# Preln attention and quantised feed-forward on one core: group 0's sums, the reciprocals and the products with them on GpSimd, and the first head outputs loaded in four pieces

## The chip, the cores and the metric

One core of a Trainium2 chip. The metric is the device time of the kernel in microseconds (us), the median of several executions. The core has TensorE (PE in the profile), VectorE (DVE), ScalarE (ACT), GpSimd (POOL), SyncE (SP), which issues all the DMAs here, and 16 DMA engines.

## The reference, cut to what matters

```python
x = residual                               # (2, 2048, 256)
xn = layernorm(x)
q, k, v = (einsum('bse,neh->bsnh', xn, W) + b for each of three W, b)      # 16 heads of 64
scores = where(q_idx < k_idx, 1e-10, q . k / 8)     # masked places count, with 1e-10
probs = softmax(scores)
x = x + einsum('bqnh,nhe->bqe', probs @ v, W_output) + Bias_output
h = layernorm(x)                           # then three blocks:
y = gelu(layernorm(qlora_linear(h))); h = qlora_linear(y) + h
out = x + h
```

A masked score is not minus infinity but 1e-10. So the denominator and the numerator have a masked part each: the number of keys after a query, and the sum of their values, times the weight of a masked place.

## The kernel before

Three stages follow one another, each a block of its own with its own semaphores: layernorm and weights, attention, feed-forward.

**Attention** works on N = 16 pairs of heads (2 batches of 8 pairs). A pair has 4 groups of 512 queries, in the order 3, 2, 1, 0, and each group its tiles of two blocks of 128 keys (`TILES`): 8, 6, 4 and 2, together NT = 20 (tiles 0 to 7, 8 to 13, 14 to 17, 18 and 19). The last two tiles of a group lie on the diagonal and are narrower (512 and 384 columns, then 256 and 128; for group 3 they stand at tiles 2 and 3). For a tile and each of the two heads, TensorE makes scores (lines 822 to 827), ScalarE takes the exponential into `probs` (line 961; three buffers, so tile t + 3 needs tile t's back), TensorE multiplies with the values into `ps_o` (line 843), and GpSimd adds the probs up over the keys in `acc` (lines 724 and 731). A tile's scores are issued one tile ahead of its product.

The order on each engine is written out by hand. A pair has 120 slots, 6 to a tile, and TensorE fits the next pair's work between its matmuls by slot (`between`): projections (`PROJ_SLOT`), score maxima (`MAX_AT`) and the list `FIN`: transposed values ("vt"), transposed maxima ("mt"), and "den", the sum of `acc` over the partitions by a matmul with ones (line 793). These share three banks of PSUM, `ps_bg`. For group 0 no engine adds up first: at slot 120 `denominators` sums the probs of both tiles directly with ones (line 799). GpSimd's loop ends with the last tile of group 1. In the last pair VectorE does the additions (`add_last`).

From the sums to the output, for each group: ScalarE copies the sums to `den_rows` (926); SP fetches them into the square form `den_sq` of 32 x 32 (`take_den`, 555); VectorE adds the masked part and takes the reciprocal (`invert`, 1043 and 1047) at `INVERT_SLOT`; SP writes it out (`put_inverse`, 561) and spreads it over the partitions (`spread_inverse`, 570); VectorE multiplies the numerator with it (`normalise`, 1055) at `NORMAL_SLOT`; SP stores (`store_heads`, 576). `take_numerator` (1035) frees `ps_o`; `num` has two buffers. GpSimd also makes the masked numerator (`masked_part`, 703) and denominator (694). SP's order is one fixed list.

**Feed-forward** works on 8 chunks of 512 rows, two at a time. SP loads the output weights `wo` (1 MB), then chunk 0's head outputs (`o_in`, 2 MB) and residual, chunk 1's, and 28 small loads of weights and biases. `heads_out(0)` and `heads_out(1)` (line 1304, 64 matmul instructions each) come first; GpSimd adds the output bias to the residual (`add_bias`) once all the small loads are there.

## Time and profile before

| what | us |
|---|---|
| median of 3 runs | 2429.66 (2426.53 to 2451.3) |
| profiled execution, its own time | 2423.18 |
| its span, first to last instruction | 2421.4 |
| TensorE busy | 2247.3 |
| VectorE / ScalarE / GpSimd busy | 1421.2 / 813.6 / 1240.8 |

The attention stage lies between 106 us (first projections) and 2045 us, the feed-forward from 2051 us to the end. Busy time of TensorE is the union of its matmuls, which overlap; its idle time before an instruction is put down to what released it.

### The profile page before, as it was taken

What the parts mean: (1) busy time and instruction counts of PE and PEld (TensorE: products, weight loads), DVE (VectorE), ACT (ScalarE), POOL (GpSimd) and SP (SyncE); (2) the same over time, 40 slices, a digit from 0 to 9 for tenths busy, and PEclk for the clock granted to TensorE, in tenths of its full rate; (3) what the DMA queues carried; (4) which work ended last, traced back from release to release, by engine and by line L of the source; (5) the groups of instructions that cost most, each with busy time, mean ns of one, the idle gap of its engine ahead of it and who ended that gap; (6) DMA issues with size and microseconds to landing.
All of it is one profiled execution on the core that took longest, in us unless ns stands there. A gap on an engine that the chain in (4) does not pass through costs nothing. (4 is left out here: it accounts for less than half of the span.)

```text
span 2421.4 us, 30652 instructions
## 1 busy us (share of the span) xinstructions
PE 2247.3 (93%) x10080; PEld 1149.0 (47%) x10080; DVE 1421.2 (59%) x3782; ACT 813.6 (34%) x1166; POOL 1240.8 (51%) x1139
## 2 busy tenths in 40 slices
PE   4389999999999999999999999999999995899987
PEld 3224444444444444444444444444444442767764
DVE  3585665656665656565656565656565763265664
ACT  1113434343434343434334344434343442011111
POOL 0106666667676757575757584858584810111110
PEclk8569999999999999999999999999999998899998
DMA  4564363635354445545453536353535332521100
GB/s 122 160 157 108 83 159 80 156 95 140 102 134 111 125 122 147 130 110 134 101 140 95 151 90 152 95 147 99 147 95 141 88 93 73 193 87 61 61 18 18
DMA packets 205356, 273.61 MB, mean 113 GB/s; under 512 B 69201, under 2 KB 86801, under 8 KB 205201
## 3 DMA queue, kind: packets, MB, share of 16 engines
q1 hardware_dynamic: 205200, 271.67, 42.8%
q8 instruction: 82, 1.34, 0.2%
q14 instruction: 74, 0.60, 0.1%
HBM read 176.69 MB, written 94.63 MB: 112 GB/s over the span
## 5 line engine op out<-in xcount | busy, mean ns | idle before, releaser
L731 POOL TENSOR_TENSOR acc<-acc,probs 128x512 f32<-128x512 f32 (+1 forms) x900 | 980.7, 1125 | 377.6 <-ACT probs L961 377.6
L961 ACT ACTIVATE probs<-ps_s 128x1024 f32<-128x1024 f32 (+2 forms) x640 | 549.4, 897 | 332.5 <-PE ps_s L824 157.2
L1011 DVE TENSOR_REDUCE partial<-ps_bg 128x1 f32<-128x512 f32 x768 | 490.3, 684 | 202.8 <-PE ps_bg L766 202.4
L822 PE MATMUL ps_s<-qq,kk 128*128 128x512 f32 (+3 forms) x1280 | 573.2, 448 | 18.8 <-ACT probs L961 18.8
L843 PE MATMUL ps_o<-probs,v 128*64 128x512 f32 (+3 forms) x2560 | 537.8, 541 | 0.0
L824 PE MATMUL ps_s<-qm,kl 128*128 128x512 f32 (+3 forms) x1280 | 467.1, 365 | 0.0
L757 PE MATMUL ps_bg<-xs,w_in 128*128 128x512 f32 x768 | 364.5, 599 | 20.8 <-DMA xs<-xn_turned 18.9
L822 PEld LDWEIGHTS ps_s<-qq,kk 128*128 128x128 f32 x1280 | 243.5, 190 | 202.4 <-issue 154.3
L766 PE MATMUL ps_bg<-k_bf,q_bf 64*128 64x512 bf16 (+3 forms) x1280 | 274.5, 364 | 20.2 <-DVE split L988 10.4
L1008 DVE CUSTOM_DVE_ANT_0 junk<-ps_bg,mask_q 128x512 bf16<-128x512 f32 (+3 forms) x512 | 230.7, 485 | 104.7 <-issue 103.5
L843 PEld LDWEIGHTS ps_o<-probs,v 128*64 128x64 f32 x2560 | 155.3, 136 | 229.9 <-issue 206.0
L824 PEld LDWEIGHTS ps_s<-qm,kl 128*128 128x128 f32 x1280 | 242.5, 189 | 38.8 <-issue 21.5
L766 PEld LDWEIGHTS ps_bg<-k_bf,q_bf 64*128 64x128 bf16 x1280 | 73.6, 93 | 355.0 <-issue 295.1
L910 ACT ACTIVATE split<-ps_bg,bias 128x512 fp32r<-128x512 f32 x128 | 88.0, 688 | 440.8 <-PE ps_bg L757 440.6
L724 POOL TENSOR_TENSOR acc<-probs 128x512 f32<-128x512 f32 x90 | 113.3, 1280 | 237.5 <-ACT probs L961 237.5
L988 DVE SCALAR_TENSOR_TENSOR split<-ps_bg,bias,split 128x512 fp32r<-128x512 f32 x128 | 94.6, 739 | 202.0 <-ACT split L910 201.3
L757 PEld LDWEIGHTS ps_bg<-xs,w_in 128*128 128x128 f32 x768 | 141.6, 191 | 131.0 <-issue 117.5
L1271 POOL TENSOR_TENSOR c_rstd<-c_var,c_minus_half 128x4 f32<-128x4 f32 x32 | 35.2, 1101 | 269.5 <-DVE c_var L1435 269.5
L1304 PE MATMUL c_ps<-c_wo,c_o_in 128*128 128x256 f32 x512 | 114.9, 384 | 28.5 <-DMA c_o_in<-heads_turned 28.5
L703 POOL TENSOR_TENSOR masked_num<-v_from,e 128x512 f32<-128x512 f32 x64 | 76.9, 1201 | 112.5 <-DVE num L1035 110.9
L1304 PEld LDWEIGHTS c_ps<-c_wo,c_o_in 128*128 128x128 f32 x512 | 98.7, 194 | 42.4 <-issue 28.7
L827 PE MATMUL ps_s<-never_above,ident_bf 128*128 128x128 bf16 x512 | 118.0, 230 | 0.0
(102 smaller groups left out, 1659.0 us busy)
## 6 DMA issues: line engine op xcount, KB each, us to landing
high_and_low<-split SPq DMA_DIRECT2D x128, 512.0 KB, 5.8
qq<-high_and_low SPq DMA_DIRECT2D x64, 512.0 KB, 4.7
kk<-high_and_low SPq DMA_DIRECT2D x128, 256.0 KB, 5.5
qm<-high_and_low SPq DMA_DIRECT2D x64, 256.0 KB, 6.4
kl<-high_and_low SPq DMA_DIRECT2D x64, 256.0 KB, 6.8
e<-masked_weights SPq DMA_DIRECT2D x128, 128.0 KB, 3.0
scale<-inverse_sums SPq DMA_DIRECT2D x128, 128.0 KB, 2.9
heads_turned<-o_out SPq DMA_DIRECT2D x64, 256.0 KB, 3.1
```

The source lines that it names most:

```text
L724: g.tensor_tensor(acc[h][:, group % 2, :], pr[:, 0:CH], pr[:, CH:2 * CH], ALU.add).then_inc(added, 1)
L731: g.tensor_tensor(acc[h][:, group % 2, q0:q0 + w], acc[h][:, group % 2, q0:q0 + w], probs[h][:, probs_slot(i, t), at:at + w], ALU.add).the ...
L757: mm = pe.matmul(bank("proj", j, u), w_in[:, s, m, :], xs[:, c, s, :], start=(s == 0), stop=(s == halves - 1))
L766: pe.matmul(bank("max", j, n, h)[:, 0:w], q_bf[HEAD[h], qb * P:(qb + 1) * P], k_bf[HEAD[h], CH * u:CH * u + w], start=True, stop=True).the ...
L822: pe.matmul(out, kk[:, h, kb * P:(kb + 1) * P], qq[:, h, q], start=True, stop=False, skip_group_check=True)
L824: mm = pe.matmul(out, kl[:, h, kb * P:(kb + 1) * P], qm[:, h, q], start=False, stop=not diagonal, skip_group_check=True)
L827: mm = pe.matmul(ps_s[:, h, at:at + P], ident_bf[:, :], never_above[:, :], start=False, stop=True, skip_group_check=True)
L843: mm = pe.matmul(ps_o[64 * h:64 * h + 64, q0:q0 + w], v[:, kb, 64 * h:64 * h + 64], probs[h][:, probs_slot(i, t), at:at + w], start=first, ...
L961: nc.scalar.activation(probs[h][:, probs_slot(i, t), 0:width], ps_s[:, h, 0:width], ACT.Exp, scale=SCORE_SCALE).then_inc(p_ready, 1)
L1008: e.tensor_tensor_reduce(junk[:, k, 0:w], of, mask_q[:, CH - w:CH], 1.0, 3 * NEVER, ALU.add, ALU.max, to).then_inc(max_read, 1)
L1011: e.reduce_max(to, of, AX.X).then_inc(max_read, 1)
L1304: mm = pe.matmul(ps_y[L][:, t, :], o_in[b][:, a, t * P:(t + 1) * P], wo[:, a, :], start=(a == 0 and t % 2 == 0), stop=(a == n_pairs - 1), ...
```

## The change

- Group 0's probs are added up by GpSimd like those of the others, in `acc[h][:, 0]`: a copy of the first 128 columns, an addition of 384, then the second tile's 256 and 128. The two matmuls with ones for it move from slot 120 to slot 14 of the next pair. Line 799 goes. In the last pair VectorE does these additions.
- `invert` and `normalise` move from VectorE to GpSimd, between its tiles (`INVERT_TILE`, `NORMAL_TILE`; from 20 on they mean tiles of the next pair). The reciprocal becomes a power of -1.
- `num` has a third buffer.
- SP's list is put in another order around them; `fin_before` gives way to a table `number` of the same counts.
- In the feed-forward, `wo` and the first two chunks' head outputs are loaded in `PIECES` = 4 pieces of two head pairs with a semaphore each, and TensorE multiplies piece by piece. The output bias has its own semaphore, for which alone `add_bias` waits. TensorE waits for the small loads only ahead of the first linear layer.

```diff
-    for k in range(min(t, LAST_TILE[1] + 1)):
-        n += 2 if k == FIRST_TILE[TILES[k][0]] else 4
+    for k in range(t):
+        n += 2 if TILES[k][0] and k == FIRST_TILE[TILES[k][0]] else 4
...
-FIN = [("vt", 0, 3), ("vt", 3, 50), ("den", 3, 60), ("mt", 3, 72), ("vt", 2, 86), ("mt", 2, 96), ("den", 2, 98),
-       ("den", 1, 110), ("vt", 1, 113), ("mt", 1, 114), ("mt", 0, 119), ("den", 0, SLOTS)]
-NFIN = len(FIN)
...
-INVERT_SLOT = {3: 68, 2: 106, 1: 118, 0: SLOTS + 8}
-NORMAL_SLOT = {3: 77, 2: 115, 1: SLOTS + 7, 0: SLOTS + 17}
+INVERT_TILE = {3: 11, 2: 17, 1: NT, 0: NT + 4}
+NORMAL_TILE = {3: 13, 2: NT, 1: NT + 2, 0: NT + 6}
...
                     if i:
+                        install_chunk(i, 0)
+                        put_inverse(i - 1, 1)
                         spread_inverse(i - 1, 1)
-                        install_chunk(i, 0)
-                        take_den(i - 1, 0)
+                        store_heads(i - 1, 2)
                         install_max(i, 0)
-                        store_heads(i - 1, 1)
                     if more:
                         keep_split(i + 1, 3)
-                    if i:
-                        put_inverse(i - 1, 0)
                     load_masked(i)
                     spread_masked(i, 3)
                     if i:
+                        store_heads(i - 1, 1)
+                    if more:
+                        keep_split(i + 1, 2)
+                    if i:
+                        take_den(i - 1, 0)
+                    spread_masked(i, 2)
+                    if more:
+                        keep_split(i + 1, 1)
+                    if i:
+                        put_inverse(i - 1, 0)
                         spread_inverse(i - 1, 0)
                     if more:
-                        keep_split(i + 1, 2)
-                    spread_masked(i, 2)
+                        keep_split(i + 1, 0)
                     if i:
                         store_heads(i - 1, 0)
-                    if more:
-                        keep_split(i + 1, 1)
-                        keep_split(i + 1, 0)
...
-                    store_heads(i, 2)
...
-                    put_inverse(i, 1)
...
+                put_inverse(N - 1, 1)
                 spread_inverse(N - 1, 1)
+                store_heads(N - 1, 2)
                 take_den(N - 1, 0)
-                store_heads(N - 1, 1)
                 put_inverse(N - 1, 0)
                 spread_inverse(N - 1, 0)
...
+                def invert(i, group):
+                    n = nth(i, group)
+                    pool.wait_ge(den_sq_in, START + 32 * (n + 1))
+                    pool.wait_ge(masked_den_ready, START + i + 1)
+                    pool.wait_ge(inverse_ready, START + n)
+                    g.tensor_tensor(total[:, :, :], den_sq[:, :, :], masked_den[:, i % 2, group], ALU.add
+                                    ).then_inc(total_ready, 1)
+                    pool.wait_ge(consts, START + 1)
+                    pool.wait_ge(total_ready, START + n + 1)
+                    pool.wait_ge(inverse_kept, START + 16 * n)
+                    g.tensor_tensor(inverse[:, :, :], total[:, :, :], minus_one[:, :, :], ALU.pow).then_inc(inverse_ready, 1)
+                def normalise(i, group):
+                    n = nth(i, group)
+                    pool.wait_ge(scale_in[group % 2], START + 32 * (2 * i + (3 - group) // 2 + 1))
+                    pool.wait_ge(num_ready, START + n + 1)
+                    pool.wait_ge(o_stored[group % 2], START + 16 * (2 * i + (3 - group) // 2))
+                    g.tensor_tensor(o_out[:, group % 2, :], num[:, n % 3, :], scale[:, group % 2, :], ALU.mult
+                                    ).then_inc(o_ready, 1)
+                def between_tiles(i, t):
+                    for c in (2, 1, 0):
+                        if i and t == INVERT_TILE[c] - NT:
+                            invert(i - 1, c)
+                        if i and t == NORMAL_TILE[c] - NT:
+                            normalise(i - 1, c)
+                    for c in (3, 2):
+                        if t == INVERT_TILE[c]:
+                            invert(i, c)
+                    if t == NORMAL_TILE[3]:
+                        normalise(i, 3)
...
                 for i in range(N - 1):
                     n = 0
-                    for t in range(LAST_TILE[1] + 1):
+                    for t in range(NT):
                         group, tile = TILES[t]
...
-                            if t == MASKED_TILE[c]:
...
+                        between_tiles(i, t)
...
+                        if t == FIRST_TILE[group] and (i or group < 2):
+                            pool.wait_ge(fin_written, START + number["den", i if group < 2 else i - 1, (group + 2) % 4])
+                        if t == FIRST_TILE[0]:
+                            for h in range(2):
+                                pr = probs[h][:, probs_slot(i, t)]
+                                g.tensor_copy(acc[h][:, 0, 0:P], pr[:, 0:P]).then_inc(added, 1)
+                                g.tensor_tensor(acc[h][:, 0, P:CH], pr[:, P:CH], pr[:, CH:2 * CH - P], ALU.add
+                                                ).then_inc(added, 1)
+                            n += 4
+                            continue
...
-                masked_denominators(N - 1)
-                for c in GROUPS:
-                    masked_part(N - 1, c)
+                for t in range(NT):
+                    if t == MASKED_DEN_TILE:
+                        masked_denominators(N - 1)
+                    between_tiles(N - 1, t)
+                for t in range(NT, NT + 7):
+                    between_tiles(N, t - NT)
...
-                    if group:
-                        if i < N - 1:
-                            pe.wait_ge(added, START + POOL_OPS * i + pool_ops_before(LAST_TILE[group] + 1))
-                        else:
-                            pe.wait_ge(added_last, START + pool_ops_before(LAST_TILE[group] + 1))
-                        for h in range(2):
-                            mm = pe.matmul(to[64 * h:64 * h + 64, :], ones64[:, :], acc[h][:, group % 2, :],
-                                           start=True, stop=True, skip_group_check=True)
+                    if i < N - 1:
+                        pe.wait_ge(added, START + POOL_OPS * i + pool_ops_before(LAST_TILE[group] + 1))
                     else:
-                        for t in range(FIRST_TILE[0], NT):
-                            for kb, q0, w, at in TILES[t][1]:
-                                for h in range(2):
-                                    mm = pe.matmul(to[64 * h:64 * h + 64, q0:q0 + w], ones64[:, :],
-                                                   probs[h][:, probs_slot(i, t), at:at + w],
-                                                   start=(kb == 0), stop=(kb == 3), skip_group_check=True)
+                        pe.wait_ge(added_last, START + pool_ops_before(LAST_TILE[group] + 1))
+                    for h in range(2):
+                        mm = pe.matmul(to[64 * h:64 * h + 64, :], ones64[:, :], acc[h][:, group % 2, :],
+                                       start=True, stop=True, skip_group_check=True)
...
-                    between(i, SLOTS)
+                denominators(N - 1, 0)
...
                                         act.wait_ge(added_last, START + pool_ops_before(user % NT + 1))
-                                    if user % NT >= FIRST_TILE[0]:
-                                        act.wait_ge(fin_written, START + fin_before(i, 0))
...
                                                  scale=SCORE_SCALE).then_inc(p_ready, 1)
-                        if i and t == 0:
...
                     dve.wait_ge(p_ready, START + 2 * NT * (N - 1) + 2 * t + 2)
                     if t == FIRST_TILE[group]:
-                        if group == 1:
-                            dve.wait_ge(fin_written, START + fin_before(N - 1, fin_index("den", 3)) + 1)
-                        else:
-                            dve.wait_ge(fin_written, START + fin_before(N - 1, 0))
+                        dve.wait_ge(fin_written, START + number["den", N - 1 if group < 2 else N - 2, (group + 2) % 4])
+                    if t == FIRST_TILE[0]:
+                        for h in range(2):
+                            pr = probs[h][:, probs_slot(N - 1, t)]
+                            e.tensor_copy(acc[h][:, 0, 0:P], pr[:, 0:P]).then_inc(added_last, 1)
+                            e.tensor_tensor(acc[h][:, 0, P:CH], pr[:, P:CH], pr[:, CH:2 * CH - P], ALU.add
...
+                def load_piece(g, p):
+                    of = pairs_of(p)
+                    if g == 0:
+                        sp.dma_start(wo[:, of, :], w_out.rearrange("(a p) d -> p a d", p=P)[:, of]
+                                     ).then_inc(piece_loaded[g][p], 16)
+                    sp.dma_start(o_in[g][:, of, :], ot.rearrange("b a c p t -> b c p a t")[g // 4, 3 - g % 4][:, of]
+                                 ).then_inc(piece_loaded[g][p], 16)
...
+                for g in range(2):
+                    for p in range(PIECES):
+                        load_piece(g, p)
+                    if g == 0:
+                        sp.dma_start(b_out_row[:, :], b_out.rearrange("(o d) -> o d", o=1).to_broadcast([P, D])
+                                     ).then_inc(b_out_loaded, 16)
+                    sp.dma_start(x_in[g][:, :, :], x[g]).then_inc(x_loaded[g], 16)
                 for dst, src in loads:
                     sp.dma_start(dst, src).then_inc(w_loaded, 16)
...
+                def heads_out_by_piece(g):
+                    for p in range(PIECES):
+                        pe.wait_ge(piece_loaded[g][p], START + (32 if g == 0 else 16))
+                        for a in range(n_pairs)[pairs_of(p)]:
+                            for t in range(4):
+                                mm = pe.matmul(ps_y[g][:, t, :], o_in[g][:, a, t * P:(t + 1) * P], wo[:, a, :],
+                                               start=(a == 0 and t % 2 == 0), stop=(a == n_pairs - 1),
+                                               skip_group_check=True)
+                    mm.then_inc(y_summed[g], 1)
...
                         heads_out(c, (0, 1))
+                    if i == 0:
```

## Rows read from the trace of the kernel before

**Rows 1.** The page, part 1: busy us, share of the span, instructions of each engine
```profile
PE 2247.3 (93%) x10080; PEld 1149.0 (47%) x10080; DVE 1421.2 (59%) x3782; ACT 813.6 (34%) x1166; POOL 1240.8 (51%) x1139
```
**Rows 2.** Waits: TensorE's from 178 to 2050 us; VectorE's for DMA, whole trace
```profile
PE ps_s L822 <- ACT probs L961: 18.8, 17, 1.2
PE ps_bg L766 <- DVE split L988: 10.4, 15, 0.7
...
DVE total L1043 <- DMA den_sq<-den_rows: 140.6, 31, 6.8
```
**Rows 3.** Busy us by stretch (PE, PEld, DVE, ACT, POOL), granted clock, DMA share, GB/s
```profile
875.00:991.00 116.00, 113.97 (x524) 53.62 (x522) 70.06 (x189) 46.24 (x66) 75.69 (x69) 1.00 0.55 141
```
**Rows 4.** Line 799's instructions; timeline of TensorE at two groups of sums (start, us)
```profile
L799 PE MATMUL ps_bg<-probs,ones x256: 272/432/644, 295.9 to 2033.2; 128*64 128x512 f32 x32, 128*64 128x384 f32 x32, 128*64 128x256 f32 x32, 128*64 128x128 f32 x32
...
989.50 1.08 PE L793 MATMUL ps_bg<-acc,ones 128*64 128x512 f32 x4
990.51 0.33 PE L822 MATMUL ps_s<-qq,kk 128*128 128x128 f32 x1
...
1007.10 2.37 PE L799 MATMUL ps_bg<-probs,ones 128*64 128x512 f32 x16
1009.40 0.50 PE L822 MATMUL ps_s<-qq,kk 128*128 128x512 f32 x1
```
**Rows 5.** Groups of instructions by form: busy us, mean ns of one, idle before
```profile
L731 POOL TENSOR_TENSOR acc<-acc,probs 128x512 f32<-128x512 f32 x630 | 792.2, 1289 | 377.6 <-ACT probs L961 377.6
L731 POOL TENSOR_TENSOR acc<-acc,probs 128x384 f32<-128x384 f32 x90 | 88.5, 1006 | 0.0
L703 POOL TENSOR_TENSOR masked_num<-v_from,e 128x512 f32<-128x512 f32 x64 | 76.9, 1201 | 112.5 <-DVE num L1035 110.9 <-DMA e<-masked_weights 1.6
L996 DVE CAST k_bf<-split 128x512 bf16<-128x512 f32 x64 | 47.0, 734 | 0.0
L731 POOL TENSOR_TENSOR acc<-acc,probs 128x128 f32<-128x128 f32 x90 | 39.9, 465 | 0.0
L994 DVE CAST q_bf<-split 128x512 bf16<-128x512 f32 x64 | 31.6, 494 | 0.0
L134 POOL TENSOR_TENSOR a_rstd<-a_var_eps,a_minus_half 128x4 f32<-128x4 f32 x8 | 8.1, 1011 | 72.1 <-DVE a_var_eps L159 72.1
```
**Rows 6.** Timeline of GpSimd from group 1's first tile (idle time before in brackets)
```profile
977.23 2.53 POOL L724 TENSOR_TENSOR acc<-probs 128x512 f32<-128x512 f32 x2 [1.53 <-ACT probs L961]
982.61 4.98 POOL L731 TENSOR_TENSOR acc<-acc,probs 128x512 f32<-128x512 f32 x4 [2.86 <-ACT probs L961]
...
988.60 6.61 POOL L731 TENSOR_TENSOR acc<-acc,probs 128x512 f32<-128x512 f32 x8
```
**Rows 7.** Timeline and landing of den_sq, 990 to 996 us; group 1's sums on TensorE
```profile
991.24 1.21 SPq L555 DMA_DIRECT2D den_sq<-den_rows  x2
...
DMA to landing us min/median/max: 1.7/1.7/1.7
...
998.15 1.08 PE L793 MATMUL ps_bg<-acc,ones 128*64 128x512 f32 x4
```
**Rows 8.** Timeline at the end of attention
```profile
2031.17 2.32 PE L799 MATMUL ps_bg<-probs,ones 128*64 128x512 f32 x16
...
2034.44 1.13 SPq L570 DMA_DIRECT2D scale<-inverse_sums  x2
...
2037.87 0.69 DVE L1055 TENSOR_TENSOR o_out<-num,scale 128x512 f32<-128x512 f32 x1 [4.69 <-DMA scale<-inverse_sums]
...
2045.01 0.34 SPq L576 DMA_DIRECT2D heads_turned<-o_out  x1
```
**Rows 9.** Timeline at the start of the feed-forward
```profile
2051.08 0.41 SPq L1235 DMA_DIRECT2D c_wo<-in_L_attn_W_output  x1
...
2062.01 29.36 PE L1304 MATMUL c_ps<-c_wo,c_o_in 128*128 128x256 f32 x128 [28.52 <-DMA c_o_in<-heads_turned]
...
2096.14 1.94 PE L1316 MATMUL c_ps<-c_ident,c_z 128*128 128x128 f32 x8 [4.77 <-DVE c_z L1444]
```

More of the change, by code:

```diff
@@ L326, in background @@
             order += [(kind, pair_of(i, kind, c), c) for kind, c, at in FIN
-                      if at == n and pair_of(i, kind, c) < n_pairs_in_all]
-    first, users, counts = {}, [], {"proj": 0, "max": 0, "fin": 0}
+                      if at == n and 0 <= pair_of(i, kind, c) < n_pairs_in_all]
+    order.append(("den", n_pairs_in_all - 1, 0))
+    first, users, number, counts = {}, [], {}, {"proj": 0, "max": 0, "fin": 0}
     for use in order:
@@ L334, in background @@
             users.append((kind, counts[kind]))
-    return first, users
+        number[use] = counts[kind]
+    return first, users, number
 FIN_FIRST = [("mt", 3), ("mt", 2), ("mt", 1), ("mt", 0), ("vt", 3), ("vt", 2), ("vt", 1)]
-NFIRST = len(FIN_FIRST)
 def attention(nc, xnt, w_qkv, b_qkv, parts, max_kept, kept, inverses, ot):
@@ L941, in _ @@
                 act.wait_ge(consts, START + 1)
[L942 to L943 removed]
+                for kind, c in FIN_FIRST:
+                    evacuate(0, kind, c)
                 for i in range(N):
```

130 lines of the change are left out of this document (48 added, 82 removed).

## The prediction, made before the changed kernel had run

> **What bounds the kernel now.** I read the page first: PE is busy for 93% of the span, POOL for 51% [rows 1]. Busy is not proof of a bound, so next the waits of PE over the attention stage, from 178 to 2050 us: of those 1870 us PE waits about 19 for ScalarE, once in a pair, and 10 for VectorE [rows 2]. Nobody keeps PE waiting; it is the list of its matmuls that takes the time. The table by stretches shows the same for 116 us in the middle of the stage: PE 113.97 us busy at full granted clock (1.00, 2.4 GHz), VectorE 70, GpSimd 75.7 [rows 3]. A pair lasts (1007.1 - 295.9) / 6 = 118.5 us, from the first start of the matmuls that add up group 0 to those of pair 6 [rows 4]. So in attention a microsecond taken off PE is a microsecond off the time, 15 times over (the last pair has no next pair to prepare and ends in a tail of its own), and a microsecond that PE must wait is one lost. In the feed-forward the start counts: PE stands still for 28.5 us, until 2062.0, for the first head outputs [rows 9].
>
> **Part 1, group 0's sums leave PE.** Before, line 799 makes them with 16 matmul instructions a pair; these begin at 1007.10 and the next scores at 1009.40, 2.30 us. The other groups' sums (line 793, 4 instructions) begin at 989.50 and the next scores at 990.51, 1.01 us [rows 4]. The new group 0 is of that second kind. PE gains 1.29 us a pair, 15 x 1.29 = **-19.4 us**. They also move from the end of the pair to slot 14 of the next, where they wait for GpSimd's last addition of group 0: by my reckoning below it is done within some 6 us of the pair's end, and PE comes there about 20 us after it. This wait costs nothing. ScalarE's copy of the sums moves along.
>
> **Part 2, what GpSimd gets.** By the rows of one form [rows 5] an addition takes 1289 ns at 512 columns and 465 at 128: 2.15 ns a column and 0.19 us for the rest. In each pair are new: two copies of 128 columns (no row has one; between 0.19, the fixed part, and 0.465, an addition; 0.4 taken), two additions each of 384, 256 and 128 columns (1.01, by the line 0.74, and 0.47): 5.2 us. Four products like line 703's, 4 x 1.20 = 4.8. Four additions of 32 columns at 0.19 + 32 x 0.00215 = 0.26: 1.0. And four reciprocals as a power of -1 over 32 columns. Together 11.0 us + 4 P, with P the time of one power.
>
> **P is the open term.** The only power in the trace has 4 columns and takes 1.01 us (line 134) [rows 5], of which an ordinary instruction would need 0.20; 0.81 us is the power's own. If all of it is a fixed cost, P is 1.0 us; if it goes with the columns, 0.20 us each, P is 0.19 + 32 x 0.205 = 6.7 us. These are the ends. I take **P = 2 us**, near the lower: 0.8 us spent on 4 columns is more easily a start-up and a few steps in flight than 32 times a lone step, but no row has a second width, and this is the weakest point of the sum. At 2 us GpSimd's load is 77 + 19 = 96 of 117 us, and it fits on average. What counts is where it queues.
>
> **Part 3, the place where a late GpSimd meets PE.** PE adds up group 1 (line 793 again) at slot 110, 998.15 in pair 6 [rows 7], and now waits there for an engine with more to do. The new step ahead of it is the reciprocal of group 2, set before tile 17's additions. Its input: SP issues the two copies of the sums at 991.24, the second about 0.6 later, and they land after 1.7 us [rows 7], at 993.5. GpSimd's run of 8 additions from 988.60 takes 6.61 us [rows 6]; its first four, tile 16's, cost two of 512 and two of 384 columns, 4.4 us back to back, and end at 993.0. Then 0.26 + P, then tile 17's four, 2.2 us: done at 993.5 + 0.26 + P + 2.2 = 996.0 + P. Against 998.15 this leaves **2.1 us for P**, with a tenth lost to each of the two hand-overs some 2.0. At P = 2 the wait is just covered; every microsecond beyond is lost 15 times. Further up, at tile 11, stands group 3's reciprocal and at tile 13 a product: 1.5 us + P more before GpSimd's two idle stretches of 1.53 and 2.86 us [rows 6], 4.39 in all. So for P up to 2.9 it has caught up before tile 16; beyond that this excess is added to the other.
>
> The remaining ones lie at tiles 20 to 26, that is 0 to 6 of the next pair. ScalarE needs tile t's probs free at tile t + 3, three tiles or some 17 us later; GpSimd may be blocked there for the landing of group 1's sums (VectorE now waits up to 6.8 us for such landings [rows 2]) and still meet that. The new waits on the queues: behind GpSimd's wait for a landing stand its own additions only; SP's wait for the reciprocal now comes after the installation of chunk 0, so that is issued sooner, and what stands behind it (the next split chunk, needed at tile 3, 20 us on) has room. store_heads and the third numerator buffer take a wait for the product off VectorE; it was none that PE saw, so nothing is gained. VectorE loses its 4 x 0.7 us of products and its waits for landings: nothing either, it is not the bound.
>
> **Part 4, the tail.** Before: PE's last sums begin at 2031.17 and the last store is issued at 2045.01; one spread-out of the inverse to the product takes 2037.87 - 2034.44 = 3.43 us [rows 8]. After, PE finishes 1.3 us sooner, but in SP's queue the fetch of group 0's sums stands behind group 1's reciprocal, its spread-out and a store, and reciprocals and products are slower. Followed with 1.4 us for addition and reciprocal: group 1's put at 2035.0, spread at 2036.8, group 0's sums fetched at 2038.3, in at 2040.9, inverted at 2042.8, spread at 2044.6, in at 2048.1, product 1.2: last store at 2049.3, +4.3 us. With P = 2 each of the two reciprocals adds 1: **+6.3 us**.
>
> **Part 5, the heads in pieces.** Before, one load of 1 MB and one of 2 MB, the first issued at 2051.08, have to be in before PE starts at 2062.01 [rows 9]: 3 MB in 10.9 us, of which some 8 are transfer (0.39 MB a us) and some 3 latency. A quarter is 2 us of transfer: PE can start at about 2056, 6 us sooner. It needs some 3.5 us for a piece at full clock and twice that at the half clock at which it comes out of the idle stretch; pieces land every 2 us, so it never waits again. Its 128 instructions, 29.4 us, are the same [rows 9], and everything behind (PE's first transpositions at 2096) moves with them: **-6 us**, between -2 (if the later load of chunk 2, issued behind more small loads, becomes late) and -7. The bias's own load and the later wait for the weights are needed so that VectorE can follow; they cost nothing, as VectorE starts on chunk 0 only when PE is done with it.
>
> **The sum.** -19.4 + 0 + 6.3 - 6.0 = **-19.1 us** against the profiled execution, whose own time is 2423.2 (span 2421.4). The median of the runs shown is 2429.7, 6.5 more; taken off that: **2410 us**, -0.8%. Changes within 1% (24 us) are about what a measurement of this kernel can't tell from none, and this forecast lies just inside.
>
> **A rule against the change.** Line 703's product takes GpSimd 1.20 us [rows 5], VectorE's takes 0.69 [rows 8]. The Trainium skill, "GPSIMD Engine Reference", section "Engine selection", says that two-input elementwise work belongs on VectorE, GpSimd being about twice as slow: the rows agree, at 1.7. By that rule the four products would cost a pair 2 us more; by the waits only the tail's last one is on the path.
>
> **Rivals.**
> *The power goes with its columns*, P = 6.7. For it: 4 x 0.2 explains the one row fully. Against: nothing but my guess of a start-up. Then PE waits at slot 110 of each pair 4.7 + 3.8 = 8.5 us; it decides from P = 3 on, where the wait (1.1) eats the 1.3 gained. Time: -19.4 + 15 x 8.5 + 4.3 + 2 x 5.7 - 6 = +118: 2548 us, slower.
> *The power lies between*, P from 2.3 to 3.5: waits of 0.3 to 2.1 us a pair, +5 to +32, tail +1 to +3 more: 2416 to 2445, no difference.
> *VectorE gets slower.* Its casts of the same size take 494 and 734 ns on average [rows 5], and the slower one stands where PE waits 0.7 us a pair for VectorE's split. The Trainium skill, "GPSIMD Engine Reference", section "Specifications", says the two engines share their SBUF interfaces, with contention when VectorE has two SBUF inputs; the rows of casts fit a contention but don't show it. With GpSimd busy for a quarter more of the time, this 0.24 us could strike at two or three more places where PE is close behind: +1 to +1.5 us a pair, +15 to +22. 2425 to 2432, no difference.
>
> **Chances.** Forecast 0.62, own range 2400 to 2422; power between 0.15; power by columns (P above 3.5) 0.15; slow VectorE 0.08. The range that leaves out 2 in 10 takes the forecast's, both no-difference rivals and omits the power by columns: 2398 to 2445. Faster by over 1% (under 2405.4): the forecast with the copies and waits at their lower ends, and the median's 6 us above the profiled execution gone, 0.30. Slower by over 1%: the power by columns and the upper end of "between" with a slow VectorE, 0.19. Within: 0.51.
>
> **What would show it.** Line 799 gone, the interval between the sums of one group in neighbouring pairs down from 118.5 to 117.2; the power's row, which decides: under 2 us and PE's waits stay near 2 us a pair; above, a new row PE ps_bg <- POOL acc at line 793, as many microseconds as P exceeds 2. The last store of attention 20 us (before: 13.8) after the start of PE's last sums. First head matmul 5 us after SP's first load instead of 11. The prediction is wrong if the power is long, if tile 16's additions end late, or if VectorE's split makes PE wait more than 1 us a pair.

## The result, and the profile after

The changed kernel takes **2612.9 us** (median of 4 runs, 2593.8 to 2637.0) against 2432.7 of the kernel before in the same series: ratio 1.070, 95% interval 1.059 to 1.081. 2410 was forecast, in a range of 2398 to 2445: wrong in sign and size. One of the four runs, the 2637.0, was in a slower state; the ratio leaves it out and compares 2602.4, the median of the other three. The profiled execution has 2602.4 us, a span of 2600.6 and a mean granted clock of 0.937 (before: 2421.4 and 0.968).

The page, part 1, of the changed kernel, beside [rows 1]:

```profile
PE 2276.7 (88%) x9888; PEld 1150.9 (44%) x9888; DVE 1374.1 (53%) x3599; ACT 814.8 (31%) x1166; POOL 1753.3 (67%) x1451
```

TensorE has 192 instructions fewer and yet 29 us more busy time: its instructions took longer, so the clock fell. GpSimd has 512 us more. Its groups by form (busy us, mean ns of one, idle time before) show what was added:

```profile
L716 POOL TENSOR_TENSOR inverse<-total,minus_one 32x32 f32<-32x32 f32 x64 | 347.5, 5430 | 8.5
L724 POOL TENSOR_TENSOR o_out<-num,scale 128x512 f32<-128x512 f32 x64 | 84.2, 1316 | 28.9 <-DMA scale<-inverse_sums 28.9
...
L757 POOL TENSOR_TENSOR acc<-probs 128x384 f32<-128x384 f32 x30 | 29.6, 986 | 0.0
L711 POOL TENSOR_TENSOR total<-den_sq,masked_den 32x32 f32<-32x32 f32 x64 | 16.1, 251 | 87.2 <-DMA den_sq<-den_rows 87.2
L756 POOL COPY acc<-probs 128x128 f32<-128x128 f32 x30 | 8.4, 280 | 0.0
```

The first row is P: **5.43 us**, not 2. Product, copy and small addition are within 0.12 us of what was estimated. TensorE's waits, beside [rows 2] (in total, times, longest):

```profile
PE ps_bg L833 <- POOL acc L771: 93.4, 15, 6.6
PE ps_s L855 <- ACT probs L993: 50.7, 33, 2.2
...
PE ps_bg L808 <- DVE partial L1038: 17.1, 20, 9.5
```

Three rows, three losses. The first is the one the prediction named as its test: TensorE at the sums' line waits for GpSimd. The second was 18.8 us, 17 times, before; a second wait per pair has come. The third has one wait of 9.5 us in it. The timeline of GpSimd and of TensorE where the first one falls (start, us; idle time before in brackets):

```profile
1184.11 4.43 POOL L771 TENSOR_TENSOR acc<-acc,probs 128x512 f32<-128x512 f32 x4
1188.50 0.24 POOL L711 TENSOR_TENSOR total<-den_sq,masked_den 32x32 f32<-32x32 f32 x1
1188.87 5.43 POOL L716 TENSOR_TENSOR inverse<-total,minus_one 32x32 f32<-32x32 f32 x1
1194.28 2.21 POOL L771 TENSOR_TENSOR acc<-acc,probs 128x256 f32<-128x256 f32 x4
```
```profile
1196.64 1.97 PE L833 MATMUL ps_bg<-acc,ones 128*64 128x512 f32 x4 [6.58 <-POOL acc L771]
1204.93 0.47 PE L855 MATMUL ps_s<-qq,kk 128*128 128x512 f32 x1 [1.16 <-ACT probs L993]
...
1210.81 0.50 PE L855 MATMUL ps_s<-qq,kk 128*128 128x512 f32 x1 [2.17 <-ACT probs L993]
```

In order: tile 16's additions, group 2's sum and power, tile 17's additions, and then at once group 1's sums on TensorE. That is the order of Part 3. The sums take 1.97 us where they took 1.08. The table by stretches tells why (TensorE's busy time, granted clock, DMA share, GB/s):

```profile
1187.00:1190.00 3.00, 3.00 (x24) 1.00 0.00 0
1190.00:1193.00 3.00, 0.06 (x1) 1.00 0.00 0
1193.00:1196.60 3.60, 0.00 (x0) 0.50 0.01 1
1196.60:1203.00 6.40, 6.36 (x19) 0.50 0.83 223
1203.00:1209.00 6.00, 4.49 (x26) 0.98 0.36 71
```

Some 3 us into the wait the granted clock has gone from 1.00 to 0.50 (2.4 to 1.2 GHz), and it stays there for 6.4 us of work after it: 3.2 us lost behind a wait of 6.6. This is one of the dearer pairs. Behind the 15 waits for GpSimd the work at half clock lost 1.8 to 3.4 us each, 2.6 on average. The shorter wait of 2.17 us at the turn of the pair was followed by half clock in 6 of 15 pairs, 1.7 us lost each time, 0.7 a pair on average.

A **period**, from group 1's sums to those of the next pair, is 118.2 to 118.9 us before and 127.9 to 130.7 after, with one of 139.0. For a typical pair: 6.4 (wait) + 2.6 + 0.7 (clock, in the two places) + 0.9 (the new wait at the turn of the pair, less the matmuls saved; first experiment) = 10.6, and 118.5 + 10.6 = 129.1. Over the whole: the last sums start 170.0 us later (2201.21 for 2031.17), from there to the feed-forward's first load it takes 34.6 us for 19.9 (+14.7), and from that load to the end of the span 364.9 for 370.3 (-5.4). 170.0 + 14.7 - 5.4 = 179.3; the two spans differ by 179.2.

### The profile page after: what moved, and what is told of

Read it like the earlier page. It is cut to its first block and busy times, and to the rows that moved or that the text cites. A ratio compares the mean times of both kernels' runs of the same rounds, so it can differ in the third digit from the quotient of the medians.

```text
span 2600.6 us, 30428 instructions
## 1 busy us (share of the span) xinstructions
PE 2276.7 (88%) x9888; PEld 1150.9 (44%) x9888; DVE 1374.1 (53%) x3599; ACT 814.8 (31%) x1166; POOL 1753.3 (67%) x1451
## 5 line engine op out<-in xcount | busy, mean ns | idle before, releaser
L771 POOL TENSOR_TENSOR acc<-acc,probs 128x512 f32<-128x512 f32 x960 | 1016.9, 1089 | 238.3 <-ACT probs L993 238.2
L855 PE MATMUL ps_s<-qq,kk 128*128 128x512 f32 (+3 forms) x1280 | 581.1, 454 | 50.7 <-ACT probs L993 50.7
L876 PE MATMUL ps_o<-probs,v 128*64 128x512 f32 (+3 forms) x2560 | 554.0, 555 | 0.0
L857 PE MATMUL ps_s<-qm,kl 128*128 128x512 f32 (+3 forms) x1280 | 472.4, 369 | 0.0
L799 PE MATMUL ps_bg<-xs,w_in 128*128 128x512 f32 x768 | 369.7, 607 | 19.1 <-DMA xs<-xn_turned 19.1
L716 POOL TENSOR_TENSOR inverse<-total,minus_one 32x32 f32<-32x32 f32 x64 | 347.5, 5430 | 8.5
L799 PEld LDWEIGHTS ps_bg<-xs,w_in 128*128 128x128 f32 x768 | 142.7, 192 | 129.1 <-issue 118.8
L833 PE MATMUL ps_bg<-acc,ones 128*64 128x512 f32 x256 | 82.5, 726 | 94.6 <-POOL acc L771 93.4
L960 ACT COPY den_rows<-ps_bg 128x512 f32<-128x512 f32 x64 | 37.5, 587 | 235.0 <-PE ps_bg L833 229.6
```

What stands on the lines that cost most here:

```text
L716: g.tensor_tensor(inverse[:, :, :], total[:, :, :], minus_one[:, :, :], ALU.pow).then_inc(inverse_ready, 1)
L771: g.tensor_tensor(acc[h][:, group % 2, q0:q0 + w], acc[h][:, group % 2, q0:q0 + w], probs[h][:, probs_slot(i, t), at:at + w], ALU.add).the ...
L799: mm = pe.matmul(bank("proj", j, u), w_in[:, s, m, :], xs[:, c, s, :], start=(s == 0), stop=(s == halves - 1))
L855: pe.matmul(out, kk[:, h, kb * P:(kb + 1) * P], qq[:, h, q], start=True, stop=False, skip_group_check=True)
L857: mm = pe.matmul(out, kl[:, h, kb * P:(kb + 1) * P], qm[:, h, q], start=False, stop=not diagonal, skip_group_check=True)
L876: mm = pe.matmul(ps_o[64 * h:64 * h + 64, q0:q0 + w], v[:, kb, 64 * h:64 * h + 64], probs[h][:, probs_slot(i, t), at:at + w], start=first, ...
```

## The experiments

Twelve kernels besides the changed one, in three series with the kernel before running beside each (its medians there: 2443.7, 2437.6 and 2435.1). "Power" says what takes the reciprocal. "Period" is the usual one, in us. Three kernels leave something out: multiply_for_power takes no reciprocal at all, power_16_columns and power_16_scan_first only that of one head in two.

| run | power | time, us | ratio to before (95%) | period |
|---|---|---|---|---|
| changed kernel | GpSimd, 32 columns | 2612.9 | 1.070 (1.059 to 1.081) | 129 |
| recip_on_vector | VectorE's reciprocal | 2441.3 | 0.998 (0.996 to 1.001) | 119.3 |
| all_on_vector | VectorE's reciprocal | 2453.8 | 1.005 (1.003 to 1.008) | 120.2 or 121.9 |
| pieces_only | VectorE's reciprocal | 2437.7 | 0.998 (0.996 to 1.001) | 118.2 to 122.1 |
| power_later | GpSimd, 32 columns | 2643.8 | 1.081 (1.076 to 1.086) | 131 to 137 |
| multiply_for_power | none | 2436.8 | 1.000 (0.998 to 1.002) | 119.3 |
| power_16_columns | GpSimd, 16 | 2620.4 | 1.073 (1.069 to 1.077) | 130 to 134 |
| power_on_128_lanes | GpSimd, 8 | 2480.2 | 1.016 (1.013 to 1.020) | 119.5 to 121 |
| mt0_moved | VectorE's reciprocal | 2425.4 | 0.995 (0.993 to 0.997) | 118.4 |
| power_16_scan_first | GpSimd, 16 | 2522.6 | 1.037 (1.033 to 1.041) | 124 to 126 |
| lanes_scan_first | GpSimd, 8 | 2475.6 | 1.016 (1.012 to 1.020) | 120.5 or 122.1 |
| mt0_slot8 | VectorE's reciprocal | **2406.1** | **0.989 (0.985 to 0.992)** | 117.2 |
| lanes_scan_mt8 | GpSimd, 8 | 2439.5 | 1.000 (0.998 to 1.003) | 118.4 to 120 |

### First series: which part costs it

**recip_on_vector**: only the reciprocals (addition and reciprocal) go back to VectorE. Three stand at their old slots; group 0's stands at slot 24 of the next pair instead of 8, because its sums now come at slot 14.

```diff
-INVERT_TILE = {3: 11, 2: 17, 1: NT, 0: NT + 4}        # GpSimd: power
+INVERT_SLOT = {3: 68, 2: 106, 1: 118, 0: SLOTS + 24}  # VectorE: e.reciprocal
```

> The changed kernel with the addition and the reciprocal of invert back on VectorE (its RECIPROCAL, at the old slots); the products stay on GpSimd. Theory 1, the long power: the power of 32 columns takes 5.4 us at GpSimd and makes PE wait 6.6 us a pair at group 1's sums, and the wait brings the half clock. Without it that row of waits is gone, the clock is 1.00 all through attention and the span falls by 160 us or more. Theory 2, the lost cover: taking line 799 away uncovers a wait of 2.2 us of PE for ScalarE at the pair's start, so of the 1.3 us that it was to bring nothing is left; then the span is 2421 + 15 x 0.9 - 5.5 (pieces) + 3 (tail) = 2432. If the cover was not lost: 2412. Theory 3, GpSimd has simply too much (its load and the shared use with VectorE): over 2460 even so.

2441.3 us: no row for GpSimd is left in TensorE's waits, and the loss is gone. The one row that stays is the second of the three:

```profile
PE ps_s L837 <- ACT probs L975: 50.1, 31, 2.2
```

Period 119.26, so 0.9 over before, where -1.3 was forecast. ScalarE's timeline at the turn of the pair, in this kernel:

```profile
1139.39 0.25 ACT L937 CAST rows<-ps_bg 8x128 fp32r<-8x128 f32 x1 [1.67 <-PE ps_bg L796]
1139.68 0.31 ACT L948 ACTIVATE rows<-rows 8x128 f32<-8x128 f32 x1
1140.02 0.40 ACT L951 ACTIVATE rows<-rows,masked_bias 8x128 f32<-8x128 f32 x1
1140.44 1.94 ACT L975 ACTIVATE probs<-ps_s 128x1024 f32<-128x1024 f32 x2
```

The row of maxima of group 0 ("mt" 0, slot 119) makes three small steps, 1.05 us, directly ahead of the exponentials that TensorE's next scores wait for. Before, TensorE was doing line 799's matmuls over just this time, 2.3 us at 1007.10 [rows 4].

**all_on_vector**: the products go back to VectorE too.

> As recip_on_vector, and the products back on VectorE as well: only group 0's sums stay on GpSimd, with the three buffers, SP's new order and the pieces. Theories 1 and 2: same as recip_on_vector within 3 us of span (2430), for the products were never what PE waited for. Theory 3: clearly faster than recip_on_vector, by 10 us or more.

A miss for all three theories: 1 and 2 had expected no difference, 3 a gain, and the kernel is 12 us slower than recip_on_vector. VectorE's product, two operands in SBUF, takes 1.08 us here (0.75 in the kernel before), and TensorE waits for maxima behind line 1009 for 9.5 us, 18 times (1.3 us, 4 times, in recip_on_vector). These 64 instructions, at these slots (group 1's and 0's are later than in the kernel before), are better off on GpSimd.

```profile
L1053 DVE TENSOR_TENSOR o_out<-num,scale 128x512 f32<-128x512 f32 x64 | 68.9, 1076 | 19.9 <-DMA scale<-inverse_sums 19.9
```

**pieces_only**: the kernel before with nothing but the new start of the feed-forward.

> The kernel before with the new feed-forward stage alone (output weights and head outputs of two chunks in four pieces). All theories: attention as before, span 2421.4 - 5.5 = 2416, PE's first head matmul 4.5 us after SP's first load (before: 10.9). If the pieces were part of the loss: above 2421.

First load to first matmul 5.0 us (before: 10.9), first load to the end 364.3 (370.3): -6.0. The forecast of Part 5 holds for this stage. In the medians it is -0.2%, within what can be told from none. The span expected, 2416, did not come: it is 2431.4, because the attention stage, which the edit does not touch, ended 15.5 us later than in the profile of the kernel before (periods of 118.2 to 122.1 for 118.2 to 118.9). The kernel before itself took 2433 to 2458 us in this series. So the span decides nothing here; the stretch of the feed-forward does.

**power_later**: the power of group 2 one tile later, behind tile 17's additions (`INVERT_TILE = {..., 2: 18, ...}`).

> The changed kernel with group 2's power one tile later, at tile 18 and so behind tile 17's additions, on which PE's sums of group 1 wait. Nothing else. Theory 1 (the place counts, not the load): PE's wait at group 1's sums falls from 6.6 to about 1 us a pair, the half-clock stretches go with it, span 2440 to 2470. Theory 3 (the load counts): GpSimd is as full as before, the wait only moves to ScalarE's probs, span above 2560.

A miss. The wait at the sums fell to 0.8 us at most, and these came for it:

```profile
PE ps_bg L808 <- DVE partial L1041: 62.9, 11, 10.8
PE ps_bg L808 <- DVE vt L1013: 49.4, 8, 8.8
```

TensorE waits for VectorE, and VectorE has no wait for GpSimd in this profile. It is VectorE's casts that are held up. Each takes 0.42 us as a rule; here 24 of them take 2.3 to 11.9, and all 128 together 242 us for 89 in the changed kernel. One of them, with GpSimd beside it and TensorE behind it:

```profile
1152.02 4.93 POOL L771 TENSOR_TENSOR acc<-acc,probs 128x512 f32<-128x512 f32 x4
1153.34 11.21 DVE L1024 CAST q_bf<-split 128x512 bf16<-128x512 f32 x1
1156.91 1.25 POOL L702 TENSOR_TENSOR masked_num<-v_from,e 128x512 f32<-128x512 f32 x1
1158.13 4.91 POOL L771 TENSOR_TENSOR acc<-acc,probs 128x512 f32<-128x512 f32 x4
1163.01 1.25 POOL L724 TENSOR_TENSOR o_out<-num,scale 128x512 f32<-128x512 f32 x1
```
```profile
1165.20 0.61 PE L808 MATMUL ps_bg<-k_bf,q_bf 64*128 64x512 bf16 x1 [10.78 <-DVE partial L1041]
```

The cast starts inside a run of GpSimd without a gap and ends at 1164.55, 0.3 us after the last of the rows shown; GpSimd's next and last instruction of the run, at 1164.22, has 32 partitions. The maxima stand behind it, and TensorE behind them. By these rows the new place of the power shifted GpSimd's runs onto the casts; no run with a gap at the casts was made to show it. When this run was planned, only the queue behind the old place had been looked at.

### Second series: is it the power's length?

**multiply_for_power**: `ALU.pow` becomes `ALU.mult` in the same place.

> The changed kernel with a multiplication by -1 in the place of the power in all four groups, at the same places of GpSimd's list; it leaves out the reciprocal, nothing else. The instruction should take 0.25 us, like the addition ahead of it, instead of 5.43. Theory 1 (the power's length alone makes TensorE wait at the sums of groups 2 and 1; the other 11 us of new GpSimd work fit): that wait falls from 6.6 us a pair to under 0.5, the half-clock stretches go with it, the pair's period falls from 129 to 119.3 us (118.4 of before plus the 0.9 us that TensorE now waits for ScalarE at the turn of the pair), and the time comes to 2435 to 2446, as in the run with the reciprocals on VectorE. Rival (GpSimd is overloaded whatever the power costs, or its hand-overs are what is late): a wait of 1 us or more a pair stays in the rows for GpSimd, and the time stays over 2455.

The reciprocal is left out; its place in the list stays. The instruction takes 0.253 us, the period is 119.27, and the time 2436.8 is within 5 us of recip_on_vector. GpSimd's other 11 us of new work a pair cost TensorE nothing. **The power's length is the loss**: by the two ratios, 1.070 and 1.000, some 170 us.

**power_16_columns**: the power over one head's 16 columns, a multiplication over the other's, whose reciprocal is left out.

> The changed kernel with the power over the first head's 16 columns only and a multiplication over the second head's 16: it leaves out the second head's reciprocal. If the power goes by its columns (1.01 us at 4, 5.43 at 32: 0.38 + 0.158 a column) the instruction takes 2.9 us, with the multiplication 3.2. GpSimd works without an idle stretch from group 3's reciprocal to group 2's in the changed kernel, so theory 1 (each microsecond of either power comes back at that wait until GpSimd has caught up) takes 2 x 2.2 off the 6.6 us wait: 2.1 us are left, too short for the clock to fall; period 121.5, time 2470 (2460 to 2480). Rival A (only group 2's own power counts, the other is caught up in idle time): 4.3 us stay, with the clock's loss a period of 125 and 2520 to 2550. Rival B (the power has a large fixed part or another law, so that 16 columns cost about as much as 32): the time stays over 2570.

The most instructive miss. The power takes 2.91 us and the wait at the sums is 31.7 / 15 = 2.1 us a pair, both as theory 1 had it, and still the kernel is as slow as with 32 columns. TensorE's first row of waits, and VectorE and GpSimd where its longest ones fall:

```profile
PE ps_bg L811 <- DVE partial L1041: 100.4, 28, 8.5
```
```profile
1197.97 0.85 POOL L774 TENSOR_TENSOR acc<-acc,probs 128x128 f32<-128x128 f32 x2
1198.41 9.86 DVE L1057 TENSOR_TENSOR_SCAN v_from<-ones_row,v_from,vt 128x512 f32<-128x512 bf16 x1
1198.79 2.48 POOL L767 TENSOR_TENSOR acc<-probs 128x512 f32<-128x512 f32 x2
1201.23 4.91 POOL L774 TENSOR_TENSOR acc<-acc,probs 128x512 f32<-128x512 f32 x4
1206.11 1.08 POOL L703 TENSOR_TENSOR masked_num<-v_from,e 128x512 f32<-128x512 f32 x1
```

VectorE's scan, 1.28 us in the kernel before (64 times, none over 1.29), takes **9.86**. It starts while GpSimd is busy and ends at 1208.27, 1.08 us after GpSimd's run ends at 1207.19. The maxima that TensorE needs stand behind it. 13 of the 15 scans at this slot are this long (9.03 to 10.34). In the changed kernel there is one, 11.32 us at 1430.89, again to 1.1 us after GpSimd's first idle moment: this is its pair of 139.0 us and its wait of 9.5. Yet there too all 15 start inside a run of GpSimd without a gap. Ten of them took 1.4 us and four 2.4 to 3.3, each let in between two of GpSimd's instructions, the second of which took 1.63 us for 0.72. So the run is needed for a long scan but doesn't bring one by itself. The shorter power shifted the run: in 10 of the 13 long cases the scan starts beside additions of 512 columns, in the changed kernel mostly beside those of 256. That this decides is not shown; the one long scan of the changed kernel starts like ten short ones.

Theory 1 also called a wait of 2.1 us "too short for the clock to fall". The waits of 2.17 us at the turn of the pair, followed by half clock in 6 of 15 pairs of the changed kernel, speak against that.

The Trainium skill, "SBUF — State Buffer", section "SBUF: two separate sides", says that the two engines share a pair of ports as an exclusive lock when VectorE has two SBUF inputs, held for a whole instruction. The trace agrees that the scan is held up, but not for one instruction: here it stood through seven more of them.

**power_on_128_lanes**: nothing left out, the denominators (total, inverse and the masked ones too) laid out as 128 partitions of 8 columns.

```diff
-        den_sq = sb("den_sq", [32, 2, 16])
+        den_sq = sb("den_sq", [P, 2, 4])
...
-den_rows[64 * h:64 * h + 1, :].rearrange("o (p e) -> o p e", e=16)
+den_rows[64 * h:64 * h + 1, :].rearrange("o (p e) -> o p e", e=4)
```

> The changed kernel with nothing left out, the denominators laid out as 128 partitions of 2 x 4 instead of 32 of 2 x 16, so that the power has 8 columns: 0.38 + 8 x 0.158 = 1.65 us instead of 5.43, if what counts is columns and not elements. Theory 1: GpSimd's wait at the sums is gone, the period falls to 119.3 and the time to 2435 to 2448. Rival (the power goes by elements, which are as many as before): 5.4 us and 2590 and more. Rival 2 (copies in 16-byte pieces land later): the power is short but GpSimd waits longer for the denominators and TensorE behind it 1 us or more a pair, 2455 to 2480.

```profile
L716 POOL TENSOR_TENSOR inverse<-total,minus_one 128x8 f32<-128x8 f32 x64 | 105.7, 1651 | 8.5
```

The same 1024 elements, 3.3 times faster: it goes by columns. But 2480, not 2448: three scans of about 9 us, twelve of 1.7 to 2.9, some with small waits behind, and a tail of 27.8 us where multiply_for_power has 19.5. Rival 2 has a point in the tail: SP's write of the inverse, in smaller pieces now, lands after 2.6 us (median; 1.4 in the changed kernel).

**mt0_moved**: recip_on_vector, with group 0's row of maxima turned at slot 4 of its own pair; SP's fetch of it moves along (not shown).

```diff
-       ("den", 1, 110), ("vt", 1, 113), ("mt", 1, 114), ("mt", 0, 119)]
+       ("den", 1, 110), ("vt", 1, 113), ("mt", 1, 114)]
-FIN = [("vt", 0, 3), ("den", 0, 14), ("vt", 3, 50), ("den", 3, 60), ("mt", 3, 72), ("vt", 2, 86), ("mt", 2, 96), ("den", 2, 98),
+FIN = [("vt", 0, 3), ("mt", 0, 4), ("den", 0, 14), ("vt", 3, 50), ("den", 3, 60), ("mt", 3, 72), ("vt", 2, 86), ("mt", 2, 96), ("den", 2, 98),
```

> On top of the run with the reciprocals on VectorE: the row of maxima of group 0 is turned at slot 4 of its own pair instead of slot 119 of the one before, so ScalarE no longer has its three small steps between the last exponentials of a pair and the first of the next. Theory (TensorE's new wait of 2.2 us a pair for probs at the turn is this chain, which the 2.3 us of group 0's sums used to cover): the wait at the turn is gone, the period falls from 119.3 to 117.2 us, and the time from 2441 to 2405 to 2412, the gain of 1.29 us a pair that was forecast for the sums plus what had been hidden behind them. Rival (the exponentials of the first tile are late for another reason, such as group 0's last scores or the conversion of V): the wait stays at 1 us or more and the time at 2425 to 2441.

Half: the wait went from 2.2 to 1.2 us, the period to 118.4. At slot 4 the three steps still stood directly ahead of the next exponentials, with a little more of TensorE's work beside them.

### Third series: the cures

**power_16_scan_first**: power_16_columns, and GpSimd waits at tile 14 until the scan is done.

```diff
+                        if t == FIRST_TILE[1]:
+                            pool.wait_ge(sums_ready, START + 4 * (i + 1) + 2)
```

> The run with the power over 16 columns (it leaves out the second head's reciprocal), and one wait more: before its first addition of group 1 (tile 14) GpSimd waits until VectorE's scan of V (128x512, set at slot 86) is done, which leaves a stretch without GpSimd work for the scan. In that run the scan took 9 to 10 us instead of 1.28 in 12 of 14 pairs, always while GpSimd went without an idle stretch from one instruction to the next, and ended about 1.1 us after GpSimd had stopped; TensorE then stood some 8 us for VectorE's maxima. Theory (VectorE's scan can't get through while GpSimd works without a break): the scan is back at 1.3 to 1.8 us, the waits for maxima fall from 100 to under 10 us, GpSimd reaches the sums about 1.3 us later than by the power alone, 3.4 us of wait a pair; period 122.7, time 2480 to 2510 instead of 2620. Rival (the long scan is a symptom, for example VectorE waits for something of TensorE's or ScalarE's, and GpSimd's load as such costs the time): scans stay long somewhere, or TensorE waits elsewhere, and the time stays over 2570.

```profile
L1059 DVE TENSOR_TENSOR_SCAN v_from<-ones_row,v_from,vt 128x512 f32<-128x512 bf16 x64 | 84.7, 1323 | 1.7
```
```profile
PE ps_bg L838 <- POOL acc L776: 44.1, 15, 3.6
...
PE ps_bg L813 <- DVE partial L1046: 1.0, 3, 0.3
```

GpSimd gets a wait more, and the kernel is some 90 us faster (ratio 1.037 for 1.073). The scans are at 1.3 us, the waits for maxima gone, 2.9 us a pair wait at the sums. A gap in GpSimd's run is enough to keep the scans short. The time is 13 us above the upper end expected, which had left out the clock: it took 30 us between 300 and 1900 us (table below).

**lanes_scan_first**: the same wait with the power on 128 x 8.

> The power on 128 partitions x 8 columns (1.65 us, nothing left out) and the same wait of GpSimd for the scan ahead of tile 14. Theory (the 40 us that this kernel still lost are three pairs with a scan of 9 us and small waits for maxima in the others): no scan over 1.8 us, all pairs at 119.3 to 120, 2437 to 2450, level with the run that multiplies. Rival (the scan's wait only moves the loss to the sums: GpSimd, held 1.3 us, comes late there): a wait for GpSimd of about 1 us a pair and 2455 to 2465.

The rival is right in kind: all scans at 1.28 us, 1.3 us a pair of wait at the sums instead. 2475.6 is no better than without. Periods are 120.5 or 122.1, and the 1.6 between them is a stretch of half clock at the turn of the pair, behind the wait of 2.17 us.

**mt0_slot8**: as mt0_moved, but slot 8, and SP fetches it behind the first split chunk.

> As the run with the row of maxima of group 0 turned in its own pair, but at slot 8 instead of slot 4, and its fetch by SP behind the first split chunk. At slot 4 ScalarE's three small steps still stood directly ahead of the exponentials that TensorE waits for (1.2 us a pair instead of 2.2). At slot 8 ScalarE has 5 us without work. Theory: this wait goes, only the 1.16 us stays that the kernel before has too; period 118.4 - 1.2 = 117.2, the forecast of the sums' own gain; 2405 to 2412. Rival (SP's queue, now held until slot 8, brings the split chunks and the masked weights late): the period stays at 118.4 or grows, with waits for DMA behind the split or at the masked denominators.

```profile
PE ps_s L840 <- ACT probs L978: 17.7, 16, 1.2
```

The second wait is gone, the period is 117.17, and **2406.1 us is 1.1% faster than before** (ratio 0.989, 0.985 to 0.992), the fastest kernel of this study, some 200 us ahead of the changed one. That Part 1's gain of 1.29 us a pair exists is shown; it needed the row of maxima out of the way.

**lanes_scan_mt8**: all on GpSimd as in the change, with the three cures.

> All on GpSimd as the change has it, with the three cures together: power on 128 x 8, GpSimd waiting for the scan ahead of tile 14, maxima of group 0 turned at slot 8 of their own pair. If the three losses are independent, the period is 117.2 to 117.8 and the time 2407 to 2420, faster than before by the forecast's amount. If GpSimd's load is itself a loss, it stays 1 us a pair or more behind the run with the reciprocals on VectorE.

2439.5, 33 us behind mt0_slot8: 1.3 us a pair at the sums (19.6, 15 times), some waits for maxima (5.8, 12 times), and a tail of 27.1 us for 20.2. In this kernel the reciprocals are better off on VectorE.

**What the clock takes.** For each kernel TensorE's windows of 1 us from 300 to 1900 us, added up: idle time, and half of the time that it was busy at half clock.

| kernel | TensorE idle, us | lost to half clock, us |
|---|---|---|
| before | 29 | 0 |
| mt0_slot8 | 28 | 0 |
| multiply_for_power | 59 | 2 |
| lanes_scan_first | 73 | 14 |
| power_16_scan_first | 88 | 30 |
| changed kernel | 141 | 43 |
| power_16_columns | 167 | 45 |

## Why the prediction was wrong, point by point

**The step that failed is "P is the open term".** P was taken as 2 us between ends of 1.0 and 6.7; it is 5.43. Four widths now give one line: 1.01 us at 4 columns [rows 5], 1.65 at 8, 2.91 at 16, 5.43 at 32: 0.38 + 0.158 a column. (The row of line 134 was not the only power before: line 1271 has another of 4 columns, 1.10 us. Both have an exponent of -0.5, not -1, and neither gave a second width.) The argument "more easily a start-up" had nothing behind it; the upper end, 0.205 a column, was the nearer. With both ends open and 15 pairs behind them, the choice of 2 us carried the sign, and a chance of 0.15 for the other end was far too small. The rival *the power goes with its columns* had the mechanism, the place and the row. It gave 8.5 us of wait a pair at P = 6.7; its rule at P = 5.43, (3.4) + (5.43 - 2.9 = 2.5), gives 5.9, and 6.3 to 6.6 was measured. Its +118 us would have been +76 at that P (88.5 of waits instead of 127.5, 8.9 in the tail instead of 11.4); 179 came. Of the rest 5 us are the longer waits (93.4 in all) and most are three things that were in no sum:

- **The clock.** 2.6 us a pair behind the wait and 0.7 at the turn, some 50 over 15 pairs.
- **"TensorE gains 1.29 us a pair; this wait costs nothing"** (Part 1). The matmuls taken out had covered ScalarE's chain ahead of the first exponentials. Without them TensorE waits 2.2 us there: +0.9 net instead of -1.3, 33 us over 15 pairs. For each edit that adds work the prediction asked what hides it; for the one that removes work it never asked what that work hid. mt0_slot8 shows both halves.
- **VectorE.** The rival *VectorE gets slower* was right that a fuller GpSimd hurts VectorE, and wrong in size and, for this kernel, in place. Its casts went only from 494 to 590 and from 734 to 802 ns on average, and TensorE's wait for the split stayed at 10.4 us. One scan went from 1.28 to 11.3 us (10 us lost); 13 did in power_16_columns. Its casts were the right place in power_later, at up to 11.9 us.

**Part 2's other terms hold**: copy 0.28 (0.4), addition of 384 columns 0.99 (1.01), addition of 256 0.83 (0.74), product 1.32 (1.20), small addition 0.25 (0.26), and multiply_for_power shows that they cost TensorE nothing. **Part 3** named the place rightly. **Part 4**: +6.3 forecast, +14.7 measured. With P at 5.43 its own rule gives 4.3 + 8.9 = 13.2, near by luck, for two errors cancel. The queue's new order costs nothing: from the last sums to the feed-forward's first load it is 19.5 us in multiply_for_power, 19.9 before. So the +4.3 was wrong. And the power stands in that chain three times, not twice: group 2's, at 2193.38, keeps SP from fetching group 1's sums until 2201.41, 3.4 us after they are copied out. **Part 5**: -6 forecast, with the first head matmul 5 us after the first load; it comes after 4.4, and the stretch gives -5.4 in the changed kernel and -6.0 alone.

With P off GpSimd and the maxima moved, the profiled execution of mt0_slot8 has a span 18.5 us below before; the sum had said 19.1. That is partly luck: its last sums start 15.3 us sooner, of 19.4 expected, the tail costs 0.3 instead of 6.3, and the pieces give 3.5 instead of 6.

## What to carry to other kernels

When an operation's cost is known at one size only and it stands in a loop, give both ends near-equal chances, and work the answer out at each end. A power on GpSimd costs by its columns (5.43 us at 32, 1.65 at 8), so lay it over more partitions or, better here, leave it to VectorE's reciprocal (0.34 us for the same 32 x 32). Before counting matmuls as saved, read the timelines of the other engines over the very microseconds in which they ran. And GpSimd filled without a gap can hold up VectorE: keep a gap where VectorE has a short operation that TensorE waits for.

## What the runs showed of the hardware that I had not expected

- A power on GpSimd takes 0.38 us + 0.158 a column at the four widths measured, two on 128 partitions (4 and 8 columns) and two on 32 (16 and 32); a multiplication of 32 columns takes 0.25.
- A scan of VectorE with two operands in SBUF, 1.28 us alone, can be held up by a GpSimd that goes without a gap from instruction to instruction: 8.9 to 12.4 us in 18 scans of four kernels, each ending 1.08 us after GpSimd's first idle moment. In the changed kernel it mostly gets in between two of GpSimd's instructions (14 of 15 at the slot in question, 1.4 to 3.3 us; one of 2.89 at 1171.45, beside which a GpSimd addition of 256 columns took 1.63 us for 0.72). What decides which is not settled.
- A cast of VectorE, with one operand in SBUF and 0.42 us as a rule, can be held up in the same way: up to 11.9 us in power_later, and never over 1.6 us in the other kernels.
- VectorE's product, also with two operands in SBUF, went only from 0.75 to 1.08 us on average in all_on_vector.
- The granted clock of TensorE was 0.50 some 3 us into a wait of 6.6 and for 6.4 us of work after it. A wait of 2.17 us was followed by it in 6 of 15 pairs of the changed kernel and in 2 of 15 of recip_on_vector.
